# A four-layer graph network on one core: a gathered tile per block given up in two passes, and the queue ahead of them rearranged

## What is computed

```python
_loop = jnp.arange(3125)
src = concatenate([_s, _d, _loop]); dst = concatenate([_d, _s, _loop])
_o = argsort(dst, stable=True); src = src[_o]; dst = dst[_o]
...
x = layernorm(x + L0(x))   # 4 x:  x = relu((x + segment_sum(x[src], dst)) @ W1 + b1) @ W2 + b2
x = layernorm(x + L1(x))   # relu(x @ root + bias + sum_r mean over edges of kind r (8 kinds) of (x @ W[r])[src])
x = layernorm(x + L2(x))   # w_rel = comp @ weight (16 kinds); sum over edges of alphas[rel] * (x @ w_rel[rel])[src], + x @ update per edge; relu
x = layernorm(x + L3(x))   # 8 kinds: msg = (x @ W[rel])[src] + bias[rel]; sum of msg * sigmoid(msg . gw[rel] + gb[rel]); + x @ loop_weight; relu
```

## Time and profile before

| | us |
|---|---|
| runs, median of 3 | 2251.98 (2250.99 to 2253.0) |
| profiled execution | 2252.56 |
| its span | 2250.8 |
| PE, DVE, ACT, POOL busy | 1463.2, 906.3, 599.7, 1360.4 |
| POOL, 1248 gathers (line 1013) | 793.5 + 392.8 |

### The profile page before, as it was taken

How to read it: one execution, slowest core, us unless ns; L and a number is a source line. 1 busy time by engine, 2 the same in 40 slices (tenths; PEclk the granted TensorE clock), 3 DMA queues, 4 the chain that set the end, 5 groups by cost and what they waited for, 6 DMA issues and landing times.

```text
span 2250.8 us, 31616 instructions
## 1 busy us (share of the span) xinstructions
PE 1463.2 (65%) x7538; PEld 989.7 (44%) x7539; DVE 906.3 (40%) x2269; ACT 599.7 (27%) x1689; POOL 1360.4 (60%) x1574
## 2 busy tenths in 40 slices
PE   4776999999987777777764655555455433434433
PEld 2332554545456665666653533343333333323333
DVE  7887122213673444444445533333344212212212
ACT  3776000000023333333331644444343000000000
POOL 5000166720007777777777777777777777777775
PEclk8888999999988989989897876667677756565565
DMA  1000011100213333333333222222222222222221
GB/s 31 0 0 10 15 9 12 11 3 0 59 54 109 94 113 112 95 112 110 95 113 97 72 81 79 71 80 79 71 81 84 56 56 56 55 56 56 55 56 46
DMA packets 126652, 137.49 MB, mean 61 GB/s; under 512 B 80706, under 2 KB 97866, under 8 KB 123433
## 3 DMA queue, kind: packets, MB, share of 16 engines
q0 software_dynamic: 40896, 81.94, 13.9%
q1 hardware_dynamic: 85673, 54.54, 8.1%
HBM read 91.88 MB, written 44.52 MB: 61 GB/s over the span
## 4 chain that ended last, share of the span: by engine, by line
POOL 50%; PE 21%; issue 18%; ACT 5%; DVE 2%; ACTq 1%; DMA 1%; POOLq 1%; SPq 0%; DVEq 0%
POOL adj L1013 49%; PE acc L1315 18%; ACT adj L1714 5%; PE misc L1251 1%; PE acc L1586 1%; PE acc L1202 1%; ACTq L1707 1%; DVE adj L2607 0%; DMA adj<-table,adj 0%; DVE adj L2606 0%; ACTq L1714 0%; POOLq L1009 0%; PE acc L1251 0%; ACT adj L1773 0%; PE acc L1204 0%
## 5 line engine op out<-in xcount | busy, mean ns | idle before, releaser
L1013 POOL DMA_INDIRECT adj<-table,adj x832 | 793.5, 954 | 253.6 <-issue 252.9
L1586 PE MATMUL acc<-adj 128*128 x1760 | 364.5, 385 | 499.7 <-DMA adj<-table,adj 253.3
L1586 PEld LDWEIGHTS acc<-adj 128*128 128x128 f32 x1760 | 328.5, 285 | 560.3 <-issue 560.2
L1013 POOL DMA_INDIRECT adj<-tablex,adj x416 | 392.8, 944 | 210.9 <-issue 126.5
L1773 ACT ACTIVATE adj<-adj 128x128 f32<-128x128 f32 x832 | 264.5, 390 | 581.0 <-DMA adj<-tablex,adj 315.2
L1315 PE MATMUL acc<-adj,feat 128*128 (+1 forms) x2100 | 406.8, 354 | 8.4 <-issue 8.4
L1513 PE MATMUL acc<-adj 128*128 128x128 f32 x1664 | 245.3, 310 | 124.1 <-ACT adj L1773 113.9
L1997 DVE TENSOR_TENSOR adj<-acc,drel 128x768 f32<-128x768 f32 (+1 forms) x148 | 139.9, 948 | 423.6 <-PE acc L1586 423.3
L1513 PEld LDWEIGHTS acc<-adj 128*128 128x128 f32 x1664 | 228.8, 220 | 167.2 <-issue 167.1
L1315 PEld LDWEIGHTS acc<-adj,feat 128*128 (+1 forms) x2100 | 186.2, 98 | 217.1 <-issue 13.1
L959 POOL TENSOR_TENSOR node_rep<-node_rep,compb 128x128 f32<-128x128 f32 x128 | 58.5, 457 | 272.4 <-DMA node_rep<-in_L_gnn_weight_dram 263.5
(11 more groups left out here) (352 smaller groups left out, 1297.6 us busy)
## 6 DMA issues: line engine op xcount, KB each, us to landing
table<-adj SPq DMA_DIRECT2D x24, 1024.0 KB, 4.1
adj<-table,adj POOLq DMA_INDIRECT x834, 2.5
table<-adj SPq DMA_DIRECT2D x25, 512.0 KB, 2.9
adj<-tablex,adj POOLq DMA_INDIRECT x416, 2.5
table<-adj SPq DMA_DIRECT2D x25, 64.0 KB, 2.0
out_dram<-adj SPq DMA_DIRECT2D x24, 64.0 KB, 1.5
temp<-in_x_dram SPq DMA_DIRECT2D x4, 256.0 KB, 3.1
wrel<-node_rep SPq DMA_DIRECT2D x16, 64.0 KB
```

Of the source, the lines that this page charges most:

```text
L1013: pool.indirect_dma_start(ring[:, p_, 0:D], None, rows_, bass.IndirectOffsetOnAxis(ap=gidx[:, p_:p_ + 1], axis=0)).then_inc(msgs_in[third_ ...
L1586: last = nc.tensor.matmul(acc[:, bass.ds(blk[s], width)], hot[:, c, j, :], ring_flat[:, bass.ds(place[s], width)], start=False, stop=True, ...
```

## The change

**Emptied tiles.** In passes 2 and 3 the edges from a node to itself are no longer gathered for blocks 2 to 23 (LB = 2, LN = 22). Their row is among the products that DVE has in hand: `own_rows` picks it out of `stage` in pass 1, kind by kind, with a mask per partition and kind (16 operations of 128x128 a block), and `block_sum` of pass 2 adds it with its weight; for pass 3 `table_parts` of pass 2 adds it to the block's own part (8 operations a block). So every tile has a few holes, and tile 7 of each of these 22 turns is dissolved: its 128 edges are moved into the holes of tiles nearby, and the tile is neither gathered, scaled nor multiplied, in passes 2 and 3. Pass 1 keeps the old lists.

**The preparation** finds for each edge of a dissolved tile the hole it goes to. All of it is new. DVE: `code_lists`, `loop_nodes`, `loop_eighths`, `loop_holes` in layers 0 and 1, and `loops_taken` at turn 2 of pass 1, to which `edges_moved` goes too. POOL: three plain DMAs (`edge_codes`, and `here_i` and `behind_i`, each 128x22 single numbers with a stride), one for `firsts_b`, three times 22 indirect ones (`found_rows`) and twice 22 (`filled`). SP: a copy of every eighth edge end (`eighths`, 6640 numbers), 11 stores that clear `holes`, and 23 loads after the last scatter. At the start SP issues three more loads of edge ends (`next1_i`), POOL one subtraction (104x512) and DVE three operations for one more check; SP waits for the ends before it goes on to `compb`.

**Order.** The slices are issued 4, 3 and 9 in three layers. All of POOL's preparation is one list, and `pads()`, the clearing of the borders, was behind the slices and is now behind them and ahead of `filled(1)`.

The diff, cut to its core:

```diff
+LATE_FLAGS, LATE_SUMS, LATE_READ, LISTS_SET, NODES_SET, PLACES_SET, EIGHTS_SET, HOLES_SET = range(1, 9)
+LB, LN = 2, BLOCKS - 3
+EMPTY_AT = 7
+FROM_TILE = 31
+BEFORE, NEAR = 9, 30
...
-EARLY_SLICES = (range(0, 6), range(6, 11), range(11, 16), ())
+EARLY_SLICES = (range(0, 4), range(4, 7), range(7, 16), ())
...
+            sp.dma_start(next1_i[0:EVENQ, :], bass.AP(dst.tensor, dst.offset + 1, [[TW, EVENQ], [1, TW]])).then_inc(ends_in, 16)
...
+            hold(sp, ends_in, ENDS_IN)
+            sp.dma_start(first_list, firsts_i).then_inc(ends_in, 16)
...
+                        if z == 2 and not general:
+                            sp.wait_ge(late_counted, LISTS_SET)
+                            for g in range(KINDS_OF_LIST):
+                                sp.dma_start(by_place(holes[g]), no_hole.bitcast(I32).rearrange("p (h i) -> p h i", h=LISTS)).then_inc(ends_in, 16)
...
+                sp.dma_start(eighths[0:TILES - 1, :].rearrange("t e -> (t e)"), bass.AP(dst.tensor, dst.offset, [[P // 16, (TILES - 1) * (P // 8)], [1, 1]])
+                             ).then_inc(ends_in, 16)
...
+                sp.wait_ge(edges_out, (SWAPPED + LN) * 16)
+                sp.wait_ge(loops_in, (LISTED + 4 * LN) * 16)
+                sp.dma_start(moved[:, :, :], edges0.rearrange("(t p) w -> p t w", p=P)).then_inc(ends_in, 16)
+                for g in range(KINDS_OF_LIST):
+                    sp.dma_start(near_holes[:, g::KINDS_OF_LIST, :], by_place(holes[g])).then_inc(ends_in, 16)
+                    sp.dma_start(loop_i[:, g::KINDS_OF_LIST], loop_codes[g].rearrange("(b p) o -> p (b o)", p=P)).then_inc(ends_in, 16)
...
+            pool.wait_ge(pads_set, 4)
+            pool.wait_ge(ids_in, 12 * 16)
+            nc.gpsimd.tensor_tensor(next1_i[:, :], next1_i[:, :], ids_i[:, 0, :], ALU.subtract).then_inc(before_set, 1)
...
-                    for j in range(SIZES[c]):
+                    for j in range(SIZES[c] - (1 if c == 1 and emptied(ph, u) else 0)):
...
-            def passes(general):
+            def pads():
...
                 pool.sem_inc(key_pads, 1)
+
+            def passes(general):
+                if general:
+                    pads()
...
-                with pool.Fori(0, LAYERS // 2) as l:
-                    for q in range(SLICES // LAYERS):
-                        weights_slice(l, q)
-                pool.wait_ge(late_counted, PLACES_SET)
-                with pool.Fori(LAYERS // 2, LAYERS - 1) as l:
-                    for q in range(SLICES // LAYERS):
-                        weights_slice(l, q)
-                        edges_part(q)
-                for q in range(SLICES // LAYERS):
-                    if q < 3:
-                        edges_part(SLICES // LAYERS + q)
-                    weights_slice(LAYERS - 1, q)
+                def slices(n, upto):
+
+                    for z in range(n, upto):
+                        weights_slice(z // (SLICES // LAYERS), z % (SLICES // LAYERS))
+
+                def found_rows(o, table, at_):
+
+                    for b in range(LN):
+                        pool.indirect_dma_start(o(b), None, table(b), bass.IndirectOffsetOnAxis(ap=at_[:, b:b + 1], axis=0)).then_inc(loops_in, 16)
+
+                def emptied_tile(b):
+                    return (LB + b) * TPT + EMPTY_AT
+
+                def filled(h):
+
+                    of_half = [(h * KINDS_OF_LIST + g, g) for g in range(KINDS_OF_LIST)]
+                    for b, g in of_half:
+                        pool.indirect_dma_start(holes[g], bass.IndirectOffsetOnAxis(ap=slot_c[:, b:b + 1], axis=0), pairs[:, b, :].bitcast(I32), None
+                                                ).then_inc(edges_out, 16)
+                    for b, g in of_half:
+                        pool.indirect_dma_start(loop_codes[g], bass.IndirectOffsetOnAxis(ap=node_i[:, b:b + 1], axis=0), found[:, b:b + 1], None
+                                                ).then_inc(loops_in, 16)
+
+                slices(0, 2)
+                pool.wait_ge(late_counted, LISTS_SET)
+                pool.dma_start(edge_codes.rearrange("(p t) o -> p (t o)", p=P)[:, FROM_TILE:TILES], tile16[:, FROM_TILE:TILES]).then_inc(loops_in, 16)
+                for k, o in ((0, here_i), (1, behind_i)):
+                    pool.dma_start(o, bass.AP(dst.tensor, dst.offset + emptied_tile(0) * P + k, [[1, P], [TPT * P, LN], [1, 1]])).then_inc(edges_in, 16)
+                pool.wait_ge(ends_in, ENDS_IN + NONE_OUT)
+                pool.dma_start(firsts_b, first_list.partition_broadcast(P)).then_inc(edges_in, 16)
+                slices(2, 4)
+                pool.wait_ge(late_counted, NODES_SET)
+                found_rows(lambda b: sixteen[:, b, :], lambda b: eighths, row_i)
+                slices(4, 7)
+                pool.wait_ge(late_counted, EIGHTS_SET)
+                found_rows(lambda b: eight[:, b, :], lambda b: dst[0:E // 8 * 8].rearrange("(r e) -> r e", e=8), row_i)
+                for n in range(SWAPPED // 4):
+                    edges_part(n)
+                slices(7, 9)
+                pool.wait_ge(late_counted, HOLES_SET)
+                pool.wait_ge(loops_in, (LISTED + 2 * LN) * 16)
+                found_rows(lambda b: found[:, b:b + 1], lambda b: edge_codes, row_i)
+                pool.wait_ge(loops_in, (LISTED + 3 * LN) * 16)
+                filled(0)
+                slices(9, 16)
+                pads()
+                pool.wait_ge(edges_out, (SWAPPED + KINDS_OF_LIST) * 16)
+                pool.wait_ge(loops_in, (LISTED + 3 * LN + KINDS_OF_LIST) * 16)
+                filled(1)
                 passes(False)
...
+                        if s == EMPTY_AT and emptied(ph, t):
+                            continue
...
+                for j in range(SIZES[c] - (1 if c == 1 and emptied(ph, u) else 0)):
...
+            nc.vector.tensor_tensor(own_edge[:, :], ids_i[:, 1, :], ids_i[:, 0, :], ALU.is_equal)
...
+            dve.wait_ge(before_set, 3)
+            link(nc.vector.tensor_tensor(own_edge[:, :], next1_i[:, :], own_edge[:, :], ALU.subtract))
+            link(nc.vector.tensor_tensor(later_f[:, :], later_f[:, :], own_edge[:, :], ALU.max))
...
+                        if l == 0 and c == 3 and not general:
+                            loop_nodes()
+                        if l == 1 and c == 3 and not general:
+                            loop_holes()
...
+            def loop_nodes():
+
+                dve.wait_ge(edges_in, 3 * 16)
+                at_ = LB * TPT + EMPTY_AT
+                mine, next_ = (firsts_b[:, at_ + k:at_ + k + (LN - 1) * TPT + 1:TPT] for k in range(2))
+                place(nc.vector.tensor_tensor(ends_f, here_i, behind_i, ALU.not_equal))
...
+                for w in range(n_):
+                    last = nc.vector.tensor_tensor(flags[:, :, w], firsts_b[:, lo + w:lo + w + (LN - 1) * TPT + 1:TPT], node_f, ALU.is_le)
+                place(last)
+                place(nc.vector.tensor_reduce(tile_f, flags, AXX, ALU.add))
...
+            def loop_eighths():
+
+                dve.wait_ge(loops_in, (LISTED + LN) * 16)
+                counted_upto(sixteen, 16, place_n)
+                place(nc.vector.tensor_scalar(place_n, place_n, -1.0, None, ALU.add))
+                place(nc.vector.scalar_tensor_tensor(row_i, tile_f, 16.0, place_n, ALU.mult, ALU.add))
+                nc.vector.engine_nop().then_inc(late_counted, 1)
+
...
+            def loop_holes():
+
+                dve.wait_ge(loops_in, (LISTED + 2 * LN) * 16)
+                counted_upto(eight, 8, more_f)
...
+                place(nc.vector.tensor_copy(pairs[:, :, 0].bitcast(I32), tile16[:, first:first + (LN - 1) * TPT + 1:TPT]))
+                place(nc.vector.tensor_copy(pairs[:, :, 1], here_f))
+                nc.vector.engine_nop().then_inc(late_counted, 1)
...
+            def loops_taken():
+
+                dve.wait_ge(ends_in, ENDS_IN + HOLES_IN)
...
+                    if l == 0 and not general:
+                        code_lists()
...
+                    if l == 1 and not general:
+                        loop_eighths()
...
-                        edges_moved()
...
+                    if isinstance(t.k, int) and t.num() == LB:
+                        edges_moved()
+                        for q, t_, n, _ in HOMES:
+                            nc.vector.tensor_copy(idx8[:, t_:t_ + n], moved_i[:, q:q + n, 1])
+                        loops_taken()
                     if b.exists():
                         kind_part(b, t, 0)
                     if before.exists():
-                        table_parts(1, before)
+                        table_parts(1, before, now=False)
+                    own = before.exists() and picks(before)
                     if b.exists():
                         block_sum(1, t, b, False)
+                        if own:
+                            own_rows(before, 0, 4)
                         block_norm(1, b)
                     if more:
                         kind_hots(t, 3)
```

(41 more changed lines are left out.)

228 lines of the change are left out of this document (189 added, 39 removed).

## The result

The changed kernel takes 2303.53 us (median of 4, 2301.09 to 2307.87) against 2252.44: slower by 2.3% (ratio 1.0231, interval 1.0218 to 1.0243). Forecast were 2255 and at most 2274.

The account below looks back on a forecast made before the run. POOL's back-to-back gathers were taken as the bound from 668 us on, ACT's adjacency stage and PE's dense layers before. Terms 4.5 + 39 + 3 - 55 + 3.5 + 7.5 = +2.5 on 2252.56 gave 2255 us, range 2238 to 2274.

Follow-up runs that it names:

- v2: v1 with the `eighths` copy of 6640 single numbers issued in the middle of stage 1 instead of ahead of the first slice: 2217.29 us.
- v1: The changed kernel with 64 bytes per `loop_codes` entry and POOL's queue reordered, borders and the memset ahead of the x loads before `filled`: 2228.15 us.
- v3: v1 with the picks of the last two blocks moved behind the last block's copies at both ends of a pass: 2222.00 us.
- e8: v1's queue order with `loop_codes` as dense as in the changed kernel: 2264.18 us.
- e4: The changed kernel with slices 9 to 15 and 12 of 28 edge scatters ahead of `pads()`, all of `filled` behind it: 2315.64 us.

## What to carry to other kernels

Price a DMA three times: for the engine that issues it, for its own landing, and for the DMAs and the instruction streams that come behind it; here 11 scatters of 128 4-byte writes, each into 1 KB of DRAM, cost their issuer no more to issue than any others and whoever came next tens of microseconds (their issuer too, where it waited for them), and giving each entry 64 bytes removed that. When work is moved into an engine's idle gap, look for every instruction of that engine behind it which another engine waits for, not only for the next one on the critical path: here both the borders and a 0.2 us memset had to come first. A copy of single numbers belongs where nobody waits for the DMAs and engines beside it: the middle of stage 1 took it at a loss under 1 us (v2), in layer 0 it stopped DVE.

## What the runs showed of the hardware that I had not expected

- 11 scatters of 128 rows of 4 bytes into tables of 1 KB each land some 29 to 33 us after the last of them is issued (POOL's waits of 28.98 and 33.4 us); with 64 bytes per entry that wait is 1.9 us (in v1, v2 and v3). Why near addresses are slow isn't shown.
- While they or the 6640-number copy are under way, engines can pause with no releaser in the profile: DVE 9.7 us (3.7 in v2, without the copy), PE 6.3 and 5.4 us, ACT 20.0 us (e8), and SP's issue of one load takes 26.8 us instead of 3.4. In e8 this happens with a DMA share of 0.00, so that share is no sign of whether writes are still outstanding. A guess from the packet times is that instructions come by the same DMA engines (one packet of 16 KB on the instruction queue took 3.6 us there); that was not tested.
- ACT's pause of 4.7 us ahead of its first loop is absent in four profiles with the added start work, there in part in one (e4), and present in the other eight. It is not explained.
